# A decoder layer in one pass over 16 batches: where the choice of tokens and the turning of the context stand in a batch

## The chip, the cores and the metric

One Trainium2 chip, one core of it. The metric is the device time of the whole kernel in microseconds. The kernel before was timed in three runs. Engines are named as in the profile: PE is the matmul engine, DVE the vector engine, ACT the scalar engine, POOL the GpSimd engine, SP the engine that here issues only DMAs.

## The reference

The input x has 16 batches of 256 tokens of 128 numbers; the context has 16 batches of 1601 keys of 96 numbers. Three blocks follow each other, each on a layernorm of x and added to x:

```python
x = x + attention(layernorm(x))                     # one head of 128, 256 tokens
x = x + cross_attention(layernorm(x), ctx_768)      # 16 heads of 64, 1601 keys
x = x + ffn(layernorm(x))                           # a block on chosen tokens only
```

The third block weighs each token by `weights = x @ router_w + router_b`, takes the top 32 of 256 (`topv, topi = top_k(weights, 32)`), and processes the best 31 of them (sorted by place) with a small attention of 16 heads of 8, rotary angles and an MLP of 512. The processed tokens, times their weight, are written back to their places. The other tokens pass through: `out + x * (1 - sel_mask)`.

Nearly all of the work is the cross attention: per batch and pair of heads, scores of 2 x 256 queries against 1601 keys, an exponential, and the weighted sum of the context.

## The kernel before

**Tiles.** A batch has 104 tiles: 8 pairs of heads times 13 tiles of 128 keys. A tile (step `st`) is a pair of matmuls on PE (L593, L594) that make 128 keys x 512 queries of scores, split in a high and a low fp16 part, and an exponential on ACT (L910) into `PF`. Two tiles together are then rounded to the high part `EH` (step `round`; three of four on DVE, L1100, the fourth on ACT, L917), and POOL takes the rest, `EL = PF - EH` (step `lo`, L1599). Eight tiles after the scores, step `av` multiplies both parts with the context, `Ch` and `Cl` (L610, L612), into one PSUM bank. After 13 tiles step `norm` on DVE divides by the sum (L1142, L1146) into `Un`. `PF` holds 10 tiles, `EH` and `EL` 12.

**Around the tiles.** The work of the other blocks and of the next batch is laid between the tiles:

- For the next batch the context is scaled (`ctx_max` L1198, `sigma` L1204 to L1215, `ctx_scale` L962), split in `Ch` (ACT, L970) and `Cl` (DVE, L1225), and both are turned by a DMA of SP into `ChT` and `ClT` (step `turn_c`, L1716). Step `keys` (DVE, L1119) takes differences between the turned keys into `KD`.
- For each half head of queries a bound of the scores is found in advance: `diff` and `base` on PE (L634), a relu on ACT (L923), `fold` on DVE (L1126). One stands every three tiles. `base` and `fold` share two PSUM banks, so the next `base` waits for the `fold` before. `placemax` (PE L673, ACT L957, a DMA of SP, L1709) puts the bounds into a row of `AH`.
- `q` (PE L644, ACT L944, DVE L1135) makes the queries of a pair of heads 38 tiles ahead.
- The self attention of the next batch stands at tiles 5 to 56.
- The normalised sums are split, copied, turned by DMA (`u_split` L930, `u_copy` L1695, `u_low` L1605 on POOL's own DMA queue, `turn_u` L1700) and projected (`proj`, PE L655, DVE L1186).
- **Choice of tokens of the batch before**: `ln_stats2` and `sel_w` (DVE, tiles 26 to 31) make the layernorm and the weights. `sel_row` (PE, L776) turns the weights into a row in PSUM. Two `sel_count` steps on DVE (one for each half of the tokens: L1391 twice, L1393 once) count how many weights are larger. `sel_rank` (DVE, L1401, L1403, L1410, L1414) makes the ranks, the choosing matrix `GT` and adds the layernormed token to `X` where it is not chosen.
- The block on the chosen tokens runs once for four batches, in 22 steps at the tiles `CHOSEN_PLACES` of the four batches that follow; its first, `c_gather`, stands at tile 82 of the first and needs `GT` of all four.

**What sets the order.** There is no scheduler at run time. `plan` gives each step a tile, `whole_order` makes the list of each engine by sorting by tile, and `LATER` shifts a kind of step on one engine. Each engine works through its list in order and waits on semaphores where a step needs another engine. SP's list is its DMA queue: it too works in order. Small results on PE share one PSUM bank, number 7: each such step waits until the one before it has been read (`bank_free`, `freed`); `sel_row` holds it until both counts are done, `proj` until L1186.

Of the kernel before, what the change touches and what calls it, by code (L numbers as in the profile page):

```python
# [72 lines left out]
def self_attention(b):  # L73
    return [(k, b) for k in ("ln_stats0", "ln0", "sa_t", "sa_qk", "sa_v", "sa_s", "sa_turn", "sa_o",
                             "ln_stats1", "sa_n2", "sa_f")]
# [10 lines left out]


SA_PLACES = (5, 7, 10, 12, 30, 32, 56)
SEL_PLACE = 35
KEYS_LATER = 16  # L90
SIGMA_PLACE = 72
M_PLACE = 34
SPLIT_LATER, COPY_LATER, LOW_LATER, TURN_LATER, PROJ_LATER = 1, 2, 5, 9, 18
# [47 lines left out]
def ahead(n):  # L141

    if n == 0:
        todo = [(max(KT * hp - Q_LEAD, 5 * hp - 5), ("q", n, hp)) for hp in range(2, HP)]
        groups = FIRST_HEADS
    else:
        todo = [(KT * hp - Q_LEAD, ("q", n, hp)) for hp in range(HP)]
        firsts = [(h, KT * h // 2) for h in range(0, H, EARLY)]
        groups = [(h, h + EARLY, k - MAX_LEAD, k - ROW_LEAD - 3, k - ROW_LEAD) for h, k in firsts]
    for h0, h1, start, end, row in groups:  # L150

        for k, ht in spread(range(T * h0, T * h1), start, end):
            todo += zip((k, k + 1, k + 1), maximum(n, ht))
        todo += [(row, ("placemax", n, h0, h1))]
    return todo


def plan(b, beside):

    n = b + 1  # L160
    todo = [(k, step) for k, step in ahead(b) if k >= 0]
    if b >= 1:
        after = AV_LAG + KT + 5
        todo += [(after, ("ln_stats2", b - 1)), (after + 2, ("sel_w", b - 1)), (SEL_PLACE, ("sel_row", b - 1)),
                 (SEL_PLACE - 1, ("sel_count", b - 1, 0)), (SEL_PLACE + 3, ("sel_count", b - 1, 1)),
                 (SEL_PLACE + 13, ("sel_rank", b - 1))]
    if b == 0:
        todo += [(M_PLACE, ("m_max",)), (M_PLACE + 2, ("mtop",)), (M_PLACE + 5, ("msplit",))]
        todo += [(9, ("ln_stats0", 1)), (12, ("ln0", 1))]
        todo += [(10 + 4 * x, ("load_x", x)) for x in range(2, B)] + [(72, ("load_rest",))]  # L170
        todo += [(10, ("ctx_max", 1)), (18, ("sigma", 1)), (22, ("ctx_scale", 1))]
    if b == 1:
        todo += [(90, ("gains",))]
    if b + 2 < B:
        todo += [(SIGMA_PLACE - 14, ("ctx_max", b + 2)), (SIGMA_PLACE, ("sigma", b + 2)),
                 (SIGMA_PLACE + 1, ("ctx_scale", b + 2))]
        todo += [(97, ("ln_stats0", b + 2)), (101, ("ln0", b + 2))]
    if n < B:
        todo += [(TILES + k, step) for k, step in ahead(n) if k < 0]
        split = AV_LAG + 17 * (b == 0)  # L180
        todo += [(split - 3, ("ctx_hi", n, 0)), (split + 1, ("ctx_hi", n, 1))]
        todo += [(split + 1, ("ctx_lo", n, 0)), (split + 4, ("ctx_lo", n, 1))]
        todo += [(split + 8, ("turn_c", n, 0)), (split + 10, ("turn_c", n, 1)), (split + KEYS_LATER, ("keys", n))]
        q = [k + 9 * (b == 0) for k in SA_PLACES]
        todo += list(zip((*q[:6], q[5] + 4, q[5] + 9, q[6]), self_attention(n)[2:]))
        todo += [(q[6] + 2, ("bias", n))]
    return sorted(todo + beside.get(b, []), key=lambda x: x[0])
# [26 lines left out]
def whole_order(engine):  # L214
# [9 lines left out]
    for n in range(TOTAL + AV_LAG):  # L224
        b, k = n // TILES, n % TILES
        if k == 0 and b < B:
            todo = plan(b, groups)
        if k == AV_LAG + (29 if b == 0 else 12) and b + 2 < B:
            put(n, "load_ctx", b + 2)
        if n < TOTAL:  # L230
            put(n, "st", n)
        late = n - AV_LAG
        if late >= 2 and late % KT == 2:
            put(n, "av", late - 2)
            put(n, "av", late - 1)
        if late >= 0 and late % KT >= 2:
            put(n, "av", late)
        if late >= 0 and late % KT == KT - 1 and late // KT < B * HP - 1:
            put(n, "norm", late // KT)
        if n % 2 and ROUND_LAG <= n < TOTAL + ROUND_LAG:  # L240
            put(n, "round", n // 2 - ROUND_LAG // 2)
        if n % 2 and LO_LAG <= n < TOTAL + LO_LAG:
            put(n, "lo", n // 2 - LO_LAG // 2)
        while todo and todo[0][0] <= k and b < B:
            put(n, *todo.pop(0)[1])
        done = n - AV_LAG - (KT - 1)
        if done >= 0 and done % KT == SPLIT_LATER:
            put(n, "u_split", done // KT)
        for later, kind in ((COPY_LATER, "u_copy"), (LOW_LATER, "u_low"), (TURN_LATER, "turn_u"), (PROJ_LATER, "proj")):
            since = done - KT - later  # L250
            if since >= 0 and since % (2 * KT) == 0:
                quad = since // (2 * KT)
                put(n, kind, quad // QD, quad % QD)
# [1509 lines left out]
```

## Time and profile before

| | us |
|---|---|
| three runs | 2188.89, 2190.83, 2190.88 (median 2190.83) |
| profiled execution, own time | 2186.77 |
| its span | 2185.5 |
| PE busy | 2026.2 |
| POOL busy | 1881.3 |
| DVE busy | 1795.1 |
| ACT busy | 1754.8 |

The span is the time from the first to the last instruction in the profile. The busy time of PE is an upper figure, since matmuls overlap and their ends are modelled. The granted clock of PE is 0.992 of full speed over the span. Times given with an instruction are counted from the start of the span. A number in square brackets in a row of the timeline is the time that the engine was idle just before it, with what ended the idle time.

### The profile page before, as it was taken

Reading aid. Unit: us, or ns where it says so; the run is one execution under the profiler, and the core shown is the slowest. Engines: PE = TensorE matmul, PEld = TensorE weight load, DVE = VectorE, ACT = ScalarE, POOL = GpSimd, SP = SyncE. Lnnn points to the kernel's source line nnn. Section 1 sums busy time; section 2 is a strip of 40 time slices with the busy share of each in tenths; the row PEclk is TensorE's granted clock in tenths of the full one; section 3 lists DMA queues with packets and bytes.
Section 4 is the critical chain, followed back from the end, with each engine's and each line's share of the span. In section 5 each row is a group of like instructions: output and inputs, shape, how many; then the busy total and the mean of one; then the engine's idle time right before and its main releaser. Section 6 shows DMA issues by size and latency. Waiting matters only on the chain.

```text
span 2185.5 us, 56667 instructions
## 1 busy us (share of the span) xinstructions
PE 2026.2 (93%) x21333; PEld 1325.7 (61%) x21333; DVE 1795.1 (82%) x4371; ACT 1754.8 (80%) x2940; POOL 1881.3 (86%) x1066
## 2 busy tenths in 40 slices
PE   8899999999999999999999999999999999999997
PEld 4566566666666556666566666666665665666653
DVE  7788889798887888888797898988879788897864
ACT  6888888888887788888788788888878778888871
POOL 4798998989898888989888888898988889889990
PEclk9999999999999999999999999999999999999999
DMA  3222121121211112121131210312121121211111
GB/s 74 64 67 51 30 45 32 27 58 30 47 27 35 40 31 50 25 56 30 26 58 23 51 31 20 55 31 47 27 48 39 27 47 27 46 23 24 30 40 25
DMA packets 189262, 85.44 MB, mean 39 GB/s; under 512 B 161344, under 2 KB 186816, under 8 KB 188992
## 3 DMA queue, kind: packets, MB, share of 16 engines
q1 hardware_dynamic: 178672, 69.04, 14.9%
q0 software_dynamic: 9216, 12.59, 4.9%
q8 instruction: 171, 2.80, 0.5%
q14 instruction: 99, 0.81, 0.1%
q10 hardware_dynamic: 1104, 0.20, 0.1%
HBM read 16.46 MB, written 2.10 MB: 8 GB/s over the span
## 4 chain that ended last, share of the span: by engine, by line
PE 51%; DVE 21%; ACT 14%; issue 9%; POOL 4%; DMA 0%; DVEq 0%; ACTq 0%; POOLq 0%
PE PS L593 10%; PE PS L634 9%; PE PS L610 9%; PE PS L594 8%; PE PS L612 8%; DVE EH L1100 8%; ACT PF L910 6%; DVE over L1126 5%; POOL EL L1599 4%; ACT over L923 3%; ACT EH L917 2%; PE PS L644 2%; PE PS L655 1%; DVE KD L1119 1%; ACT ex L986 1%
## 5 line engine op out<-in xcount | busy, mean ns | idle before, releaser
L1599 POOL TENSOR_TENSOR EL<-PF,EH 128x1024 f16<-128x1024 f32 x828 | 1767.8, 2209 | 225.8 <-DVE EH L1100 93.8
L910 ACT ACTIVATE PF<-PS 128x512 f32<-128x512 f32 x1664 | 975.3, 600 | 239.1 <-PE PS L594 226.5
L610 PE MATMUL PS<-Ch,EH 128*128 128x97 f16 (+1 forms) x6656 | 751.8, 207 | 30.2 <-POOL EL L1599 27.8
L610 PEld LDWEIGHTS PS<-Ch,EH 128*128 128x128 f16 (+1 forms) x6656 | 605.3, 98 | 251.5 <-issue 95.5
L1100 DVE TENSOR_SCALAR_CACHE_REDUCE EH<-PF 128x1024 f16<-128x1024 f32 x621 | 748.7, 1210 | 8.5 <-ACT PF L910 8.5
L612 PE MATMUL PS<-Cl,EL 128*128 128x97 f16 (+1 forms) x6656 | 748.6, 207 | 0.0
L612 PEld LDWEIGHTS PS<-Cl,EL 128*128 128x128 f16 (+1 forms) x6656 | 596.3, 98 | 150.2 <-issue 3.2
L1126 DVE CUSTOM_DVE_ANT_1 over<-over,PS 128x802 f32<-128x802 f32 x512 | 505.5, 987 | 210.1 <-PE PS L634 124.4
L593 PE MATMUL PS<-AH,ChT 98*128 98x512 f16 x1664 | 637.6, 383 | 37.1 <-ACT PF L910 36.4
L594 PE MATMUL PS<-AL,ClT 96*128 96x512 f16 x1664 | 634.7, 381 | 0.0
L923 ACT ACTIVATE over<-PS 128x802 f32<-128x802 f32 x512 | 431.3, 842 | 57.2 <-PE PS L634 34.7
L593 PEld LDWEIGHTS PS<-AH,ChT 98*128 98x128 f16 x1664 | 162.7, 98 | 190.8 <-ACT PF L910 118.6
L634 PE MATMUL PS<-ChT,AH 96*128 96x401 f16 x1024 | 261.6, 336 | 10.6 <-DVE pmax L1126 10.3
L634 PE MATMUL PS<-KD,AH 96*128 96x401 f16 x1024 | 260.6, 335 | 1.5 <-ACT over L923 1.2
L917 ACT ACTIVATE EH<-PF 128x1024 f16<-128x1024 f32 x211 | 222.8, 1056 | 0.0
L594 PEld LDWEIGHTS PS<-AL,ClT 96*128 96x128 f16 x1664 | 164.2, 99 | 67.3 <-issue 0.9
L1135 DVE SCALAR_TENSOR_TENSOR AL<-PS,qscale,AH 96x512 f16<-96x512 f32 x128 | 95.3, 744 | 43.5 <-ACT AH L944 43.5
L944 ACT ACTIVATE AH<-PS,qscale 96x512 f16<-96x512 f32 x128 | 88.1, 689 | 33.6 <-PE PS L644 32.8
L644 PE MATMUL PS<-X2T,G 128*96 128x256 f16 x512 | 80.2, 280 | 22.5 <-DVE X L1186 15.2
L634 PEld LDWEIGHTS PS<-ChT,AH 96*128 96x128 f16 x1024 | 79.4, 99 | 32.1 <-DVE pmax L1126 15.8
L634 PEld LDWEIGHTS PS<-KD,AH 96*128 96x128 f16 x1024 | 80.4, 99 | 21.8 <-ACT over L923 3.5
L930 ACT ACTIVATE UHL<-Un 128x384 f16<-128x384 f32 x128 | 67.6, 528 | 16.9 <-DVE Un L1146 16.8
(261 smaller groups left out, 1572.4 us busy)
## 6 DMA issues: line engine op xcount, KB each, us to landing
UHL<-UHL SPq DMA_DIRECT2D x64, 192.0 KB, 2.2
UHL<-Un POOLq DMA_DIRECT2D x64, 192.0 KB, 3.5
Cf<-in_ctx SPq DMA_DIRECT2D x16, 576.0 KB
X<-in_x SPq DMA_DIRECT2D x16, 128.0 KB, 2.3
out_x<-X SPq DMA_DIRECT2D x16, 128.0 KB, 1.8
UT<-UHL SPq DMA_TRANSPOSE x64, 3.7
msk<-in_attention_mask SPq DMA_DIRECT2D x4, 256.0 KB, 4.4
AH<-mh SPq DMA_DIRECT2D x63, 2.0 KB
```

Of the source, the lines that this page charges most:

```text
L593: pe.matmul(o, ChT[j][0:DC + 2, t, :], AH[:, cs], start=True, stop=False)
L594: pe.matmul(o, ClT[j][0:DC, t, :], AL[:, cs], start=False, stop=True).then_inc(sg("st"), 1)
L610: pe.matmul(PS[:, 6, u0:u0 + DC + 1], EH[0:kr, r, qs], Ch[j][0:kr, t, 0:DC + 1], start=(t == 0 and q == 0), stop=False, skip_group_check=True)
L612: m = pe.matmul(PS[:, 6, u0:u0 + DC + 1], EL[0:kr, r, qs], Cl[j][0:kr, t, 0:DC + 1], start=False, stop=(t == KT - 1), skip_group_check=True)
L634: m = pe.matmul(PS[:, bank + n, 0:NKEY], AH[0:DC, ht * P:(ht + 1) * P], src[:, n * NKEY:(n + 1) * NKEY], start=True, stop=True)
L644: m = pe.matmul(PS[0:DC, kb, j * S:(j + 1) * S], G[:, part, 2 * hp + j, :], X2T[:, part, b % 2, :], start=(part == 0), stop=(part == 1))
L910: act.activation(PF[:, n % PRING, :], PS[0:KP, 4 + n % 2, :], ACT.Exp).then_inc(sg("ex"), 1)
L917: act.activation(EH[:, r - 1:r + 1, :], PF[:, f - 1:f + 1, :], ACT.Copy, scale=KEEP).then_inc(sg("eh_act"), 1)
L923: act.activation(over[:, i % 2, :, :], PS[:, 2:4, 0:NKEY], ACT.Relu).then_inc(sg("relu"), 1)
L1100: dve.tensor_scalar(EH[:, r - 1:r + 1, :], PF[:, f - 1:f + 1, :], KEEP, None, ALU.mult, ALU.add, accum_out=esum[:, r // 2:r // 2 + 1]).the ...
L1126: dve.tensor_tensor_reduce(out=o, in0=o, in1=PS[:, 0:2, 0:NKEY], scale=1.0, scalar=LEAST, op0=ALU.add, op1=ALU.max, accum_out=pmax[:, b % ...
L1599: pool.tensor_tensor(EL[:, r - 1:r + 1, :], PF[:, f - 1:f + 1, :], EH[:, r - 1:r + 1, :], ALU.subtract).then_inc(sg("lo_pool"), 1)
```

## The change

Two constants and two offsets in `plan` are changed. `sel_row` goes from tile 35 to 60, the two counts from 34 and 38 to 59 and 63 (on DVE one later: 35 and 39 to 60 and 64), `sel_rank` from 48 to 73. `turn_c` goes from tiles 16 and 18 to 13 and 15, and `keys` from 24 to 21 (in batch 0, which has 17 more, from 33, 35 and 41 to 30, 32 and 38). No instruction is added or removed.

```diff
-SEL_PLACE = 35
-KEYS_LATER = 16
+SEL_PLACE = 60
+KEYS_LATER = 13
...
-        todo += [(split + 8, ("turn_c", n, 0)), (split + 10, ("turn_c", n, 1)), (split + KEYS_LATER, ("keys", n))]
+        todo += [(split + 5, ("turn_c", n, 0)), (split + 7, ("turn_c", n, 1)), (split + KEYS_LATER, ("keys", n))]
```

`SEL_PLACE` is read by four steps:

```python
todo += [(after, ("ln_stats2", b - 1)), (after + 2, ("sel_w", b - 1)), (SEL_PLACE, ("sel_row", b - 1)),
         (SEL_PLACE - 1, ("sel_count", b - 1, 0)), (SEL_PLACE + 3, ("sel_count", b - 1, 1)),
         (SEL_PLACE + 13, ("sel_rank", b - 1))]
```

## Rows read from the trace of the kernel before

**Rows 1.** The page, part 1: busy time, share of the span, instructions.
```profile
PE 2026.2 (93%) x21333; PEld 1325.7 (61%) x21333; DVE 1795.1 (82%) x4371; ACT 1754.8 (80%) x2940; POOL 1881.3 (86%) x1066
```

**Rows 2.** The page, part 4: the chain that ended last, by engine.
```profile
PE 51%; DVE 21%; ACT 14%; issue 9%; POOL 4%; DMA 0%; DVEq 0%; ACTq 0%; POOLq 0%
```

**Rows 3.** Stretches of batch 2: length, then PE, PEld, DVE, ACT, POOL busy (instructions).
```profile
331.20:337.50 6.30, 5.14 (x58) 3.63 (x57) 5.37 (x11) 4.72 (x8) 4.60 (x3) 1.00 0.00 1
...
349.10:363.10 14.00, 12.42 (x124) 7.40 (x122) 13.04 (x40) 11.00 (x21) 13.83 (x10) 1.00 0.28 43
...
378.00:390.80 12.80, 11.85 (x136) 7.67 (x135) 9.56 (x19) 11.12 (x21) 12.80 (x8) 1.00 0.34 62
```

**Rows 4.** Timeline of POOL in batch 2: start, us, instruction, times [idle before].
```profile
323.54 10.50 POOL L1599 TENSOR_TENSOR EL<-PF,EH 128x1024 f16<-128x1024 f32 x5 [0.87 <-DVE EH L1100]
335.75 2.13 POOL L1599 TENSOR_TENSOR EL<-PF,EH 128x1024 f16<-128x1024 f32 x1 [1.70 <-ACT PF L910]
...
359.92 6.53 POOL L1599 TENSOR_TENSOR EL<-PF,EH 128x1024 f16<-128x1024 f32 x3
368.16 8.42 POOL L1599 TENSOR_TENSOR EL<-PF,EH 128x1024 f16<-128x1024 f32 x4 [1.71 <-ACT EH L917]
...
394.99 4.23 POOL L1599 TENSOR_TENSOR EL<-PF,EH 128x1024 f16<-128x1024 f32 x2 [0.20 <-PE PS L612]
399.70 6.50 POOL L1599 TENSOR_TENSOR EL<-PF,EH 128x1024 f16<-128x1024 f32 x3 [0.48 <-DVE EH L1100]
```

**Rows 5.** Timeline of DVE around the keys, in batch 0 (first row) and 2.
```profile
100.83 0.56 DVE L1119 TENSOR_TENSOR KD<-ChT 96x802 f16<-96x802 f16 x1
...
329.10 1.21 DVE L1100 TENSOR_SCALAR_CACHE_REDUCE EH<-PF 128x1024 f16<-128x1024 f32 x1
...
331.68 0.99 DVE L1126 CUSTOM_DVE_ANT_1 over<-over,PS 128x802 f32<-128x802 f32 x1 [1.36 <-PE PS L634]
...
332.60 1.88 DVE L1119 TENSOR_TENSOR KD<-ChT 96x802 f16<-96x802 f16 x1
```

**Rows 6.** Timeline of DVE at the ranking of batch 2.
```profile
364.38 0.21 DVE L1401 TENSOR_SCALAR_CACHE_REDUCE rank<-cnt 128x1 f32<-128x1 f32 x1
...
365.18 1.43 DVE L1414 SCALAR_TENSOR_TENSOR X<-X,keep 128x128 f32<-128x128 f32 x1
...
366.54 0.34 DVE L1414 SCALAR_TENSOR_TENSOR X<-X,keep 128x128 f32<-128x128 f32 x1
...
366.81 1.21 DVE L1100 TENSOR_SCALAR_CACHE_REDUCE EH<-PF 128x1024 f16<-128x1024 f32 x1
```

**Rows 7.** Groups by line, over the span: busy us, mean ns | idle before.
```profile
L634 PE MATMUL PS<-ChT,AH 96*128 96x401 f16 x1024 | 261.6, 336 | 10.6 <-DVE pmax L1126 10.3
...
L1391 DVE TENSOR_SCALAR_CACHE_REDUCE junk<-PS,X 128x256 bf16<-128x256 f32 x64 | 27.9, 473 | 0.8 <-PE PS L776 0.8
```

**Rows 8.** Timelines of DVE, SP, PE at the turning in batch 2; UT to landing.
```profile
316.67 1.44 DVE L1225 SCALAR_TENSOR_TENSOR Cl<-Ch,Cf 128x576 f16<-128x576 f16 x1
...
316.45 1.48 SPq L1716 DMA_TRANSPOSE ChT<-Ch  x1
321.91 1.44 SPq L1700 DMA_TRANSPOSE UT<-UHL  x1
...
324.24 1.91 SPq L1716 DMA_TRANSPOSE ClT<-Cl  x1
...
332.16 0.22 PE L655 MATMUL PS<-MH,UT 128*128 128x128 f16 x1
...
UT<-UHL SPq DMA_TRANSPOSE x64, 3.7
```

**Rows 9.** Timeline of DVE at tiles 70 to 77 of batch 2.
```profile
389.68 0.99 DVE L1126 CUSTOM_DVE_ANT_1 over<-over,PS 128x802 f32<-128x802 f32 x1 [2.12 <-PE PS L634]
...
394.77 0.98 DVE L1126 CUSTOM_DVE_ANT_1 over<-over,PS 128x802 f32<-128x802 f32 x1
...
397.43 0.99 DVE L1126 CUSTOM_DVE_ANT_1 over<-over,PS 128x802 f32<-128x802 f32 x1 [1.66 <-ACT over L923]
```

## The prediction

> **What bounds the kernel now.** I read the busy shares first, then the chain of waits, then one batch cut into stretches, then single instructions there. PE is busy in 93% of the span, POOL 86%, DVE 82% [rows 1], and the chain has 51% on PE, 21% on DVE, 14% on ACT [rows 2]: no engine is the bound throughout, so a place must be read by itself. I use batch 2 (its tile 0 is at about 302 us); batches 1 to 14 repeat it, those with steps of the chosen tokens with some longer gaps. The reader is to see in [rows 3] that the limit changes inside a batch. At tiles 60 to 72 POOL is busy for all of 12.80 us and DVE for 9.56: the pass on POOL that makes the low parts (EL), 2.1 us for each pair of tiles, sets the pace, and DVE has 3.2 us to spare. At tiles 24 to 28 it is the other way: 6.30 us for 4 tiles, with POOL busy for 4.60. Every idle gap of POOL is time which its queue of passes cannot get back, so I price the change by POOL's gaps. Batch 2 has one of 1.70 us at tile 27 and one of 1.71 us at tile 52 [rows 4]. The first follows the key differences (KD), the second the ranking (sel_rank); both stand in DVE's queue ahead of the rounding (EH) that POOL's next pass reads. In batches 1 to 14 the first is 1.7 us, and 2.3 us in five of them (5, 7, 9, 11, 13); the second is 1.71 to 2.0 us in batches 1 to 15.
>
> **Keys three tiles sooner.** KD is issued at 332.60 and takes 1.88 us; alone, with POOL idle, it took 0.56 [rows 5]. It ended at 334.48, 0.44 us after POOL's pass of that moment (323.54 + 10.50 = 334.04 [rows 4]). So it waits for POOL's pass and then needs 0.44 us. At tile 21 KD stands ahead of the rounding that begins at 329.10. POOL's fourth pass of the row of five ends at about 331.9, its third at 329.9. I take it that KD gets in at 329.9 and ends at 330.3; that rounding ends at 331.5, and POOL's fifth pass is held from 331.9 to 332.4 and ends at 334.5. The fold at 331.68 waited 1.36 us for PE [rows 5], so DVE had that much room; the next rounding, no longer behind KD, ends at 333.8. POOL's next pass begins at 334.5, not 335.75: 1.25 us gained in each of 14 batches, 17.5 us, and 0.6 us more in the five with the longer gap, 3 us. Bounds for a batch: 1.70 if nothing new appears, 0 if KD has to let one more pass go first (then KD ends at 332.4 and the rounding it holds at 333.6).
> [...] The row shows 0.56 alone against 1.88 beside a pass. [...] No row shows DVE waiting while POOL has its next EL pass ready.
>
> **Context turned sooner.** SP doesn't go by tiles, it goes by its queue. ChT already follows the split at once (316.45), since nothing of its queue stands between it and the wait; moving it from 16 to 13 changes no order. ClT does change: it stood behind the turning of UT (321.91) and the row maxima, and left at 324.24, though the split ended at 316.67 + 1.44 = 318.1 [rows 8]. It will leave at about 318, and the context load behind it can only go sooner. UT, now behind it, waits for the accumulation on POOL's queue; were it late by a whole issue (1.9 us), or by all 6.1 us that ClT gains, it would still be ahead of its reader or just there: the projection reads UT at 332.16, issue to landing of UT is 3.7 us, 321.91 + 3.7 = 325.6, so 6.6 us are free [rows 8]. I take 0; bounds 0 and 6.1 - 6.6, also 0. KD needs ChT alone, which landed some 9 us before 329.10.
>
> **Ranking away from tile 48.** Its instructions begin at 364.38; the addition to X (L1414) takes 1.43 us and 0.34 us, and the rounding behind it begins at 366.81, so 2.43 us [rows 6]. Again the first addition ends (366.61) 0.16 us after POOL's pass (359.92 + 6.53 = 366.45 [rows 4]). With it gone the rounding runs 364.4 to 365.6, POOL goes on at 366.5 in place of 368.16: 1.71 us gained, in 15 batches 25.7 us. Bounds 1.71 and 0.9 (if PE, busy 93%, sets a pace of its own there); I take 1.71, the gap itself.
>
> **Counting away from tiles 35 to 39.** Four comparisons of 0.473 us [rows 7] and two instructions of the same width, which I put at the same, are 2.8 us, 1.4 for each half, and a little less as they follow each other closely: 1.3. In tiles 36 to 48 POOL is busy 13.83 of 14.00 us [rows 3], so DVE's relief there gives nothing by itself; bounds 0 and 0.2. At the new place (tiles 60 and 64) DVE has 3.2 us spare in 12.80. The first count holds one rounding by 1.3 us where POOL has about 1.0 us of work in hand: 0.3 us lost. The second is taken up by the idle 2.12 us ahead of 389.68 [rows 9]. The q matmuls of tile 66 share bank 7 and now wait for the second count; they read it some 0.6 us later, with q needed 38 tiles ahead. Bounds 0 and 2.6; I take 0.3.
>
> **Ranking at tile 73.** This is the dear one. It lands behind sigma, the normalisation and a rounding, ahead of the fold at 394.77 [rows 9]. Small parts 0.8 us, to 395.6; the first addition waits for the pass begun at 394.99, to 397.1, and ends at 397.3, the second at 397.6: 2.8 us. The fold then ends at 398.5, PE's next base matmuls (0.336 us each, two that overlap [rows 7]: about 0.4) wait for it, the next fold runs 398.9 to 399.9 where it was 397.43, and the rounding ends at 401.05 rather than 399.55. POOL's pass of 399.70 [rows 4] starts at 401.1: 1.4 us lost. DVE's idle 1.66 us ahead of 397.43 has paid for the rest. Bounds 0 (the idle time covers it all) and 3.5 (one pass more to wait for, 2.1 us). Batch 15 has no folds, so 14 batches: (1.4 + 0.3) x 14 = 23.8 us lost.
>
> **Sum.** -17.5 - 3.0 - 25.7 + 23.8 = -22.4 us. Against the profiled execution's own 2186.77 us (span 2185.5, the rest lies around it) that is 2164.4. The median of the three runs is 4.1 us higher, 2190.83; from there 2168.4, and I say 2169.
>
> **Rivals.**
> A. The ranking at 73 is hidden whole, as is the counting: -46.2 us, 2145. For it: DVE idles 2.12 and 1.66 us around it [rows 9]. Against: that idle time lies on both sides of the cluster and not in it.
> B. The gains don't add: PE, busy 5.14 of 6.30 us at tiles 24 to 28 but 11.85 of 12.80 at 60 to 72 [rows 3], fills up when POOL's gaps close, or KD gives nothing and the rest cancels: -22.4 + 20.5 = -2, 2189.
> C. [...] In the new places POOL's passes stand back to back (five in a row from 323.54 and two from 394.99 [rows 4]), while at both old places POOL ran dry behind the instruction. If DVE has to let the next pass go first, the ranking costs 2.13 us more in 14 batches (+30 us) and KD's gain goes (+20.5): +28, 2219. With it in the ranking alone +7.5, 2198. It decides as soon as one addition in the ranking takes over 2 us. Against: at both old places DVE got in 0.16 and 0.44 us after the pass.
>
> **Chances.** Forecast 0.55 (its own range 2158 to 2182), A 0.12, B 0.13, C 0.20. The range takes in most of A, B, and C in the ranking alone: 2148 to 2202. About 0.2% (4.4 us) is what a measurement of this kernel can tell from no change. Faster 0.68 (forecast, A and a little of B), same 0.12, slower 0.20.
>
> **What would show it.** Right: POOL's gap at tile 27 under 0.6 us and none at tile 52; the first addition of the ranking at 1.4 to 1.9 us; a new gap of POOL of 1.5 to 2 us at tile 78 to 80; tiles 24 to 56 shorter by about 3 us, tiles 60 to 80 longer by under 2. Wrong: KD over 2.5 us, or an addition over 2 us (C); the gaps gone and the batch as long as before (B); no new gap near 79 (A). The forecast falls if the cluster at 73 makes PE wait for bank 7, where the projection of tile 77 must be added before q at 79, beyond the 1.4 us counted.

## The result and the profile after

The changed kernel took 2255.52 us (median of 4 runs, 2253.59 to 2259.72), the kernel before 2190.85 in the same comparison: ratio 1.030, 95% interval 1.0282 to 1.0318. It is 65 us slower, where 22 us faster was forecast. The profiled execution is 2253.59 us with a span of 2252.3. One execution in all the runs below, of kernel 7, had a granted clock of 0.653 and took 2865.65 us; it is left out of that kernel's time.

First the page: busy time, and the chain by engine. They answer to [rows 1, 2].

```profile
PE 2055.9 (91%) x21333; PEld 1343.6 (60%) x21333; DVE 1822.1 (81%) x4371; ACT 1747.0 (78%) x2940; POOL 1887.9 (84%) x1066
...
PE 48%; DVE 23%; ACT 14%; issue 10%; POOL 4%; DMA 1%; SPq 0%; ACTq 0%; DVEq 0%; POOLq 0%
```

PE's mean granted clock is new: 0.975 of full speed, 0.992 before. The page can't say more. Batch 2 in stretches can (the columns are those of [rows 3], then the granted clock of PE); these are tiles 24 to 28, 48 to 52, 52 to 60, 60 to 64, 72 to 76 and 76 to 80.

```profile
336.70:342.40 5.70, 5.70 (x68) 4.03 (x65) 4.57 (x13) 4.50 (x8) 5.59 (x4) 1.00 0.02 4
...
367.20:372.00 4.80, 4.80 (x67) 3.60 (x66) 4.05 (x11) 3.86 (x7) 4.80 (x3) 1.00 0.02 3
372.00:381.60 9.60, 9.60 (x104) 6.58 (x102) 8.18 (x16) 8.76 (x15) 9.15 (x6) 1.00 0.01 2
381.60:385.50 3.90, 3.62 (x46) 2.34 (x45) 3.90 (x12) 3.40 (x7) 2.87 (x3) 1.00 0.15 53
...
394.80:401.30 6.50, 5.28 (x56) 3.00 (x55) 6.25 (x26) 6.06 (x9) 6.32 (x4) 1.00 0.01 3
401.30:411.10 9.80, 6.69 (x57) 4.74 (x58) 7.07 (x14) 3.74 (x7) 5.42 (x3) 0.83 0.01 2
```

Tiles 24 to 28 are 0.60 us shorter than in [rows 3], as wanted. Tiles 76 to 80 took 4.20 us before and take 9.80: the loss is in these four tiles, and it repeats: 9.8 to 12.6 us in batches 1 to 14, where they took 4.2 to 4.9 before. Summed over these batches they take 145.7 us for 59.7; the next largest loss is 4.3 us, at tiles 64 to 72. The same instructions on DVE (start, us):

```profile
334.72 1.19 DVE L1119 TENSOR_TENSOR KD<-ChT 96x802 f16<-96x802 f16 x1
...
398.82 0.21 DVE L1401 TENSOR_SCALAR_CACHE_REDUCE rank<-cnt 128x1 f32<-128x1 f32 x1
...
399.62 1.69 DVE L1414 SCALAR_TENSOR_TENSOR X<-X,keep 128x128 f32<-128x128 f32 x1
401.24 2.20 DVE L1414 SCALAR_TENSOR_TENSOR X<-X,keep 128x128 f32<-128x128 f32 x1
403.37 0.98 DVE L1126 CUSTOM_DVE_ANT_1 over<-over,PS 128x802 f32<-128x802 f32 x1
405.40 0.99 DVE L1126 CUSTOM_DVE_ANT_1 over<-over,PS 128x802 f32<-128x802 f32 x1 [1.05 <-PE PS L634]
406.32 1.21 DVE L1100 TENSOR_SCALAR_CACHE_REDUCE EH<-PF 128x1024 f16<-128x1024 f32 x1
```

KD takes 1.19 us, not 1.88 [rows 5]. The second addition to X takes 2.20 us, not 0.34 [rows 6]. The ranking is 4.55 us long (398.82 to 403.37); before it was 2.43. POOL, then PE at the end of its wait:

```profile
329.16 12.94 POOL L1599 TENSOR_TENSOR EL<-PF,EH 128x1024 f16<-128x1024 f32 x6 [0.95 <-DVE EH L1100]
...
357.86 19.06 POOL L1599 TENSOR_TENSOR EL<-PF,EH 128x1024 f16<-128x1024 f32 x9
...
385.40 2.14 POOL L1599 TENSOR_TENSOR EL<-PF,EH 128x1024 f16<-128x1024 f32 x1 [1.03 <-ACT PF L910]
...
399.03 4.26 POOL L1599 TENSOR_TENSOR EL<-PF,EH 128x1024 f16<-128x1024 f32 x2 [0.18 <-PE PS L612]
407.67 4.25 POOL L1599 TENSOR_TENSOR EL<-PF,EH 128x1024 f16<-128x1024 f32 x2 [4.38 <-DVE EH L1100]
```

```profile
404.41 0.85 PE L634 MATMUL PS<-ChT,AH 96*128 96x401 f16 x2 [4.12 <-DVE pmax L1126]
```

Both old gaps of POOL [rows 4] are gone: six passes and nine passes stand back to back. In their place is one gap of 4.38 us. Where two passes follow each other from 399.03, the first addition ends at 401.31, 0.15 us after a pass, and the second at 403.44, 0.15 us after the next. That next pass began at about 401.12, while the first addition was ending and 0.12 us before the second was issued (401.24); it is so in batches 1 to 13 alike. The fold is then read by PE at 404.41, after 4.12 us in which PE, whose queue has the base matmuls first, does nothing. In short stretches behind that wait the clock is:

```profile
402.50:404.00 1.50, 0.00 (x0) 0.00 (x0) 1.50 (x3) 0.00 (x0) 0.79 (x1) 1.00 0.00 0
404.00:406.00 2.00, 1.59 (x6) 0.68 (x7) 0.95 (x3) 0.00 (x0) 0.00 (x0) 0.60 0.00 0
406.00:408.00 2.00, 2.00 (x22) 1.94 (x21) 1.54 (x4) 0.60 (x1) 0.33 (x1) 0.54 0.00 0
408.00:410.00 2.00, 2.00 (x26) 1.43 (x24) 1.62 (x3) 1.43 (x3) 2.00 (x2) 1.00 0.03 8
```

PE stood still for 4.12 us and was then granted half: in stretches of 0.5 us the clock is 0.50 from 404.5 to 407.5, 0.68 in the next and 1.00 from 408.0 on. Over the span, PE's waits for the fold ahead of the base matmuls are 68.5 us in 29 waits; before they were 10.3 in 15.

The turning did what was said. ClT leaves ahead of UT, UT leaves 0.8 us later in its batch, and PE's waits for it are what they were: one, of 6.1 us. SP's queue (it answers to [rows 8]):

```profile
322.06 1.48 SPq L1716 DMA_TRANSPOSE ChT<-Ch  x1
323.75 3.13 SPq L1716 DMA_TRANSPOSE ClT<-Cl  x1
328.33 1.44 SPq L1700 DMA_TRANSPOSE UT<-UHL  x1
```

### The profile page after: what moved, and what is told of

Its sections match the earlier page's. It is cut to its first block, busy times and chain, and to the rows that moved or that the text cites. A ratio compares the mean times of both kernels' runs of the same rounds, so it can differ in the third digit from the quotient of the medians.

```text
span 2252.3 us, 56667 instructions
## 1 busy us (share of the span) xinstructions
PE 2055.9 (91%) x21333; PEld 1343.6 (60%) x21333; DVE 1822.1 (81%) x4371; ACT 1747.0 (78%) x2940; POOL 1887.9 (84%) x1066
## 3 DMA queue, kind: packets, MB, share of 16 engines
q1 hardware_dynamic: 178672, 69.04, 14.9%
## 4 chain that ended last, share of the span: by engine, by line
PE 48%; DVE 23%; ACT 14%; issue 10%; POOL 4%; DMA 1%; SPq 0%; ACTq 0%; DVEq 0%; POOLq 0%
PE PS L593 9%; PE PS L634 8%; PE PS L594 8%; PE PS L610 8%; PE PS L612 7%; DVE EH L1100 7%; ACT PF L910 5%; DVE over L1126 4%; POOL EL L1599 4%; ACT over L923 3%; DVE X L1414 3%; ACT EH L917 2%; PE PS L655 2%; PE PS L644 2%; DVE Un L1146 1%
## 5 line engine op out<-in xcount | busy, mean ns | idle before, releaser
L1599 POOL TENSOR_TENSOR EL<-PF,EH 128x1024 f16<-128x1024 f32 x828 | 1774.3, 2230 | 284.9 <-DVE EH L1100 149.4
L610 PE MATMUL PS<-Ch,EH 128*128 128x97 f16 (+1 forms) x6656 | 759.5, 208 | 34.4 <-POOL EL L1599 29.7
L612 PE MATMUL PS<-Cl,EL 128*128 128x97 f16 (+1 forms) x6656 | 756.3, 208 | 0.0
L612 PEld LDWEIGHTS PS<-Cl,EL 128*128 128x128 f16 (+1 forms) x6656 | 601.7, 99 | 153.6 <-issue 10.5
L593 PE MATMUL PS<-AH,ChT 98*128 98x512 f16 x1664 | 645.1, 388 | 34.4 <-ACT PF L910 33.2
L594 PE MATMUL PS<-AL,ClT 96*128 96x512 f16 x1664 | 641.7, 386 | 0.0
L634 PE MATMUL PS<-ChT,AH 96*128 96x401 f16 x1024 | 264.8, 340 | 68.8 <-DVE pmax L1126 68.5
L634 PE MATMUL PS<-KD,AH 96*128 96x401 f16 x1024 | 261.9, 337 | 1.5 <-ACT over L923 1.2
L634 PEld LDWEIGHTS PS<-ChT,AH 96*128 96x128 f16 x1024 | 79.1, 99 | 92.3 <-DVE pmax L1126 76.0
L634 PEld LDWEIGHTS PS<-KD,AH 96*128 96x128 f16 x1024 | 80.8, 99 | 21.7 <-ACT over L923 3.4
L644 PE MATMUL PS<-X2T,G 128*96 128x256 f16 x512 | 78.9, 277 | 11.7 <-DVE junk L1393 4.8
```

Source lines behind the costliest of these rows:

```text
L593: pe.matmul(o, ChT[j][0:DC + 2, t, :], AH[:, cs], start=True, stop=False)
L594: pe.matmul(o, ClT[j][0:DC, t, :], AL[:, cs], start=False, stop=True).then_inc(sg("st"), 1)
L610: pe.matmul(PS[:, 6, u0:u0 + DC + 1], EH[0:kr, r, qs], Ch[j][0:kr, t, 0:DC + 1], start=(t == 0 and q == 0), stop=False, skip_group_check=True)
L612: m = pe.matmul(PS[:, 6, u0:u0 + DC + 1], EL[0:kr, r, qs], Cl[j][0:kr, t, 0:DC + 1], start=False, stop=(t == KT - 1), skip_group_check=True)
L634: m = pe.matmul(PS[:, bank + n, 0:NKEY], AH[0:DC, ht * P:(ht + 1) * P], src[:, n * NKEY:(n + 1) * NKEY], start=True, stop=True)
L644: m = pe.matmul(PS[0:DC, kb, j * S:(j + 1) * S], G[:, part, 2 * hp + j, :], X2T[:, part, b % 2, :], start=(part == 0), stop=(part == 1))
```

## The experiments

Theory: because the two additions read two operands in SBUF, DVE waits for POOL's passes; at tile 75 these stand back to back and each addition waits for one (1.69 and 2.20 us); the fold behind them holds PE (4.12 us), which then also loses its clock (0.50 of full speed). Rivals: the cluster at tile 73 is too long whatever the additions do; the earlier DMA costs; the two parts collide. The texts on record call the theory, and that wait for POOL, "the port": that is a name and nothing more. The runs show which instructions were held beside POOL's passes and for how long, not what the two engines share.

The kernel before was timed again in each comparison, with medians from 2188.06 to 2190.85 us. Differences between kernels of different comparisons are therefore good to some 3 us; those against the kernel before are taken within one comparison.

**1. The keys and the turning alone.** From the changed kernel:

```diff
-SEL_PLACE = 60
+SEL_PLACE = 35
```

> The turning of the context at 13 and 15 and the keys at 21, the choice of tokens left at 35 to 48. After the change KD takes 1.19 us instead of 1.88 and the gap of POOL at tile 27 is nearly gone, so this part alone should be worth what was forecast: 1.25 us in 14 batches and 3 us more, 20 us, so 2170. The rival (the earlier DMA of ClT is what costs) has this kernel slower than before, up to 2255.

2166.62 us, ratio 0.990 (0.9886 to 0.9919): 21.4 us faster than before (2188.06 in this comparison). This part of the forecast holds, in size too.

**2. The choice of tokens alone.** From the kernel before: `SEL_PLACE = 60`.

> The choice of tokens at 60 to 73, the turning and the keys left where they were. If the two parts add up, 2255.5 + 20 = 2276. In the profile both additions to X of the ranking (L1414) should again take 1.7 and 2.2 us at tile 75 and PE should wait about 4 us for the fold behind them. If instead it is the two parts together that collide, it is near before, 2190 or less.

2274.78 us, ratio 1.040 (1.0383 to 1.0414), 86.7 us slower; the additions take 1.69 and 2.20 us. The parts add up: 2188.1 - 21.4 + 86.7 = 2253.4. The collision is out.

**3. The additions with one operand from SBUF.** From the changed kernel:

```diff
-m = dve.scalar_tensor_tensor(out=X[..t..], in0=X3[..t, 0:D], scalar=keep[..t..], in1=X[..t..],
-                             op0=ALU.mult, op1=ALU.add, accum_out=spill())
+m = dve.tensor_scalar(X[..t..], X3[..t, 0:D], keep[..t..], None, ALU.mult, ALU.add, accum_out=spill())
```

> The whole change, but the two additions to X of the ranking read one operand from SBUF instead of two (X is overwritten by X3 times keep, its old value is left out), same shape, same place. Theory of the port (DVE waits for POOL's passes because it reads two operands): both take 0.34 us, the ranking 1.6 us instead of 4.6, PE waits 3 us less for the fold, and the time falls below before: 2150 to 2165. Rival (the cluster of sigma, normalisation, ranking and fold at tile 73 is too long by itself, or bank 7 holds PE): the additions are short but the time stays above 2225.

2172.03 us, ratio 0.993 (0.9912 to 0.9941). DVE, then POOL:

```profile
395.23 0.34 DVE L1414 TENSOR_SCALAR_CACHE_REDUCE X<-X,keep 128x128 f32<-128x128 f32 x1
...
395.50 0.34 DVE L1414 TENSOR_SCALAR_CACHE_REDUCE X<-X,keep 128x128 f32<-128x128 f32 x1
```

```profile
399.74 4.22 POOL L1598 TENSOR_TENSOR EL<-PF,EH 128x1024 f16<-128x1024 f32 x2 [0.88 <-DVE EH L1100]
```

Beside the same passes both take 0.34 us, and 83.5 us are gone. The gap of 4.38 us is 0.88 (L1598 here is L1599 elsewhere). The edit changes the instruction too, and not only what it reads. The changed kernel's own trace has the first instruction with one operand from PSUM in place of SBUF (its durations are the least, the median and the most, in ns):

```profile
L1186 DVE SCALAR_TENSOR_TENSOR X<-PS,pback,X x64: 475/482/485, 115.7 to 2212.9; 128x256 f32<-128x256 f32 x64
```

57 of these 64 were issued while a pass of POOL ran, and none took over 485 ns. With the 0.34 us above this points to the second operand in SBUF: the instructions with one were not held, the additions with two were. The cluster without its waits is no disaster; but the time is 7 us over the end of what was expected, so the move costs something beside these waits.

**4. PE kept busy while it waits.** From the changed kernel:

```diff
+STREAM_BUSY |= {("base", n, 2): 17 for n in range(2, B)}
```

> The whole change, with 17 idle matmuls of 512 columns (0.22 us each, 3.7 us) on PE ahead of the base matmuls that wait for the fold at tile 76, in batches 1 to 14, so that PE is busy while it waits. After the change the granted clock falls to one half for 3.4 or 6.8 us behind that wait in nearly every batch. If that fall is part of the price, the clock stays at 1.00 and 1.7 to 3.4 us of each batch come back: 2255 - 30 = 2225. If the fall costs nothing, since others are waited for then, the time stays at 2255 or a little over.

2225.76 us, ratio 1.017 (1.0156 to 1.0186). The stretch of about tiles 75 to 80 of batch 2, then PE at its wait (lines of this kernel are one higher: L635 is L634):

```profile
397.20:407.00 9.80, 9.34 (x84) 5.62 (x83) 8.60 (x14) 5.29 (x9) 5.74 (x4) 1.00 0.01 2
```

```profile
397.59 3.83 PE L565 MATMUL PS<-identb 128*128 128x512 f16 x17
401.88 0.52 PE L635 MATMUL PS<-ChT,AH 96*128 96x401 f16 x2 [0.46 <-DVE pmax L1127]
```

The additions take 1.69 and 2.20 us as before, the clock stays at 1.00, and 29.8 of the 83.5 us come back. So some 30 us of the loss are the clock, not the wait. The fillers themselves end 0.46 us before the base matmuls begin, so they cost little.

**5. The ranking one tile later.** `("sel_rank", b - 1)` at `SEL_PLACE + 14`.

> The whole change, but the ranking one tile later, at 74: DVE takes the fold of tile 73 ahead of it. Theory (the ranking of 4.6 us holds the fold, the fold holds the base matmuls of tile 76, and PE stands in its queue for 4 us and loses its clock): the base of tile 76 is no longer held, the additions still take 1.7 and 2.2 us or more, and only the next fold and POOL's pass behind the ranking are late: 2190 to 2220. Rival (what counts is that POOL runs dry behind a ranking of 4.6 us, whatever the fold does): near 2255.

2208.52 us, ratio 1.008 (1.0049 to 1.0113). DVE, then POOL:

```profile
393.81 0.98 DVE L1126 CUSTOM_DVE_ANT_1 over<-over,PS 128x802 f32<-128x802 f32 x1
...
395.51 0.79 DVE L1414 SCALAR_TENSOR_TENSOR X<-X,keep 128x128 f32<-128x128 f32 x1
...
396.24 2.21 DVE L1414 SCALAR_TENSOR_TENSOR X<-X,keep 128x128 f32<-128x128 f32 x1
```

```profile
400.64 4.21 POOL L1599 TENSOR_TENSOR EL<-PF,EH 128x1024 f16<-128x1024 f32 x2 [2.34 <-DVE EH L1100]
```

The fold now goes first, the second addition waits as long as ever, and 47 us are back. PE's waits for the fold are 10.5 us in 15 waits, as in the kernel before (the profiled execution is the fastest of the four, 2197.42 us). So what made a wait of 2 us so dear was that it stood ahead of the fold that PE needed. The edit changes one thing more: the first addition waits 0.90 us less, so the 47 us are not the place of the fold alone.

**6. The turning alone.** From the kernel before: `turn_c` at `split + 5` and `split + 7`.

> The kernel before with the turning of the context alone at 13 and 15. ClT leaves ahead of UT. As forecast it changes nothing: 2188, within 4 us. Rival: it is part of what the keys gained (ClT and the context load sooner), then 2180 or less, or it costs a little that the keys paid, then over 2195.

2188.72 us, ratio 0.9996 (0.9987 to 1.0005). It changes nothing, in either direction.

**7. The wait at the old place.** Kernel 1 with the edit of kernel 3.

> The turning and the keys three tiles sooner, the choice at 35 to 48, and the two additions to X of the ranking with one operand from SBUF (the old X is left out). It measures what the port costs at the old place: the first addition takes 0.34 us, not 1.43, so 1.1 us less in 15 batches if POOL's gap at tile 52 shrinks by as much: 2166 - 16 = 2150. If that gap is set by something else, 2166.

2151.16 us, ratio 0.982 (0.9798 to 0.9835): 15.5 us less than kernel 1, as 1.1 us in 15 batches. Against kernel 3, the same work without any of these waits, the new places cost 20.9 us. The two profiled executions (2174.58 and 2149.10 us) say where. Over batches 1 to 14, tiles 64 to 72, where the counts now stand, take 129.1 us in kernel 3 and 118.9 here. Tiles 76 to 80, behind the ranking, take 70.8 and 59.7. All other stretches together differ by some 4 us, and the counts' old place (tiles 36 to 48) by 0.1. At the new one PE waits for the second count, 4.8 us in 12 waits, since the matmuls of the queries (L644) need bank 7; here and in the kernel before they have no such wait. Behind the ranking it waits 0.91 us for the fold in each of batches 1 to 13.

**8. One addition only.** The changed kernel with `for t in range(1)` for the additions of batches 0 to 14; the second half of the tokens is left out.

> The whole change, with only the first of the two additions to X of the ranking (the second half of the tokens isn't added, in batches 0 to 14). The forecast priced the ranking at tile 73 with one wait for the port; the second addition was put at 0.34 us and took 2.2. If the second wait is the step that failed, the time falls by far more than 2.2 us a batch, since PE waits less and keeps its clock: 2172 (both additions without a wait) plus 1.35 us in 14 batches is 2191; 2215 if the clock still falls. If the first wait does the harm, it stays above 2225.

2206.51 us, ratio 1.008 (1.0046 to 1.0103); the addition takes 1.69 us, POOL's gap is:

```profile
401.55 4.24 POOL L1599 TENSOR_TENSOR EL<-PF,EH 128x1024 f16<-128x1024 f32 x2 [1.92 <-DVE EH L1100]
```

The second addition alone is worth 49.0 us. The time lies between the two that were expected, and the clock still falls (mean 0.983): PE waits 2.0 us for the fold in batches 1 to 13.

**9. The additions where POOL has run dry.** Kernel 1 with all of its work; the two additions become a step of their own (`add_kept`), on DVE behind `sel_w` of the next batch; batches 14 and 15 keep them in the ranking.

```diff
+if b >= 2: todo += [(AV_LAG + KT + 7, ("sel_add", b - 2))]     # "dve": {"sel_add": 3}
...
-for t in range(T): m = dve.scalar_tensor_tensor(...)
+if b >= B - 2: add_kept(b)
```

> All of the work, as in the kernel with the turning and the keys alone sooner (choice at 35 to 48), but the two additions to X of the ranking stand behind the weights of the next batch, at tile 31 of DVE, where POOL has run dry in every profile so far (1.98 us idle at tile 34). Theory of the port: both additions take 0.34 us there, POOL's gap at tile 52 (1.71 us) goes, the one at 34 grows by 0.6 to 0.7 us: about 1.0 us less in 14 batches, 2166.6 - 14 = 2152. Rival (an instruction on DVE costs what it takes wherever DVE is late): no gain, 2166.

2157.01 us, ratio 0.986 (0.9845 to 0.9875). POOL in this kernel (L1607 is L1599 elsewhere):

```profile
342.12 2.13 POOL L1607 TENSOR_TENSOR EL<-PF,EH 128x1024 f16<-128x1024 f32 x1 [2.52 <-DVE EH L1109]
...
350.61 19.21 POOL L1607 TENSOR_TENSOR EL<-PF,EH 128x1024 f16<-128x1024 f32 x9
```

Both additions take 0.35 us. POOL's gap at tile 34 is 2.52 us where it was 1.98, and the one at 52 is gone. Net 9.6 us less than kernel 1 (14 were expected), 31 us less than before with nothing left out: the fastest full kernel here.

**10. The same in the changed kernel.**

> The whole change with all of the work, its two additions to X likewise behind the weights of the next batch at tile 31. If the additions at tile 73 to 75 are the whole cause, the time is that of the kernel in which they had one operand from SBUF (2172), less 0.68 us of ranking at 73 that is gone, plus 0.68 us at tile 31: 2165 to 2178. If something else of the move costs too, over 2190.

2178.87 us, ratio 0.996 (0.9944 to 0.9969). Moving two instructions turns the change from 65 us slower to 9 us faster than before (2188.12). The time is 0.9 us over the end of what was expected. Against kernel 9 it is 21.9 us slower, near the 20.9 of 3 against 7. This one isn't free of the wait: the ranking in batch 15 keeps its additions, and the first takes 5.17 us, for 1.42 us in kernel 9.

## Why the prediction was wrong

- **Keys sooner, -20.5 us**: right. Measured -21.4 for keys and turning together; KD 1.19 us, where 1.2 was worked out (329.1 to 330.3), by the wait for one pass. That KD would get in behind the running pass, ahead of the next, was my estimate; no row showed it. In the changed kernel it was issued at 334.72, 0.72 us before the next pass began, and waited for the running pass alone; it is so in batches 1 to 14.
- **Turning, 0**: right (kernel 6).
- **Ranking away from tile 48, -25.7 us**: the mechanism half right, the size wrong. POOL's gap of 1.71 us did close. But PE is busy for all 9.60 us of tiles 52 to 60, and tiles 48 to 60 take 14.4 us for 14.9 before: 0.5 us, not 1.7. POOL, ahead of PE, waits for ACT's exponentials at 385.40 instead (1.03 us). Experiment 7, in which only the wait at the old place is gone, gained 1.0 us a batch. That is near my lower bound (0.9, PE's own pace), and I took the gap itself; rival B named this for the whole change, and it held for this step.
- **Counting, +0.3 us a batch**: too small. Kernel 3 against kernel 7 has 0.7 us a batch at tiles 64 to 72. I let the queries of tile 66 wait for the second count at no cost, because their result is needed 38 tiles later. But PE works in order: it stood in its queue, 0.4 us each time. In the change itself this is half hidden: against the kernel before, tiles 64 to 68 are some 0.6 us longer and 68 to 72 some 0.3 shorter.
- **Ranking at tile 73, +1.4 us a batch**: the step that failed. I let the first addition wait for the pass and put the second at the 0.34 us of [rows 6]. There POOL had run dry behind the first; here its next pass was ready and began 0.12 us before the second addition was issued, which then waited for all of it: 2.20 us. Experiments 3 and 8 show it: without the waits -83.5 us, without the second alone -49.0. The signs that I had named say the same: the first addition took 1.69 us, within the 1.4 to 1.9 of a right forecast; the second was over 2 us, the sign of rival C; and the new gap of POOL was 4.38 us, not 1.5 to 2.
- **What a wait there costs.** Rival C had the mechanism (a further pass, 2.13 us) at 30 us for the ranking. The wait did decide, as C said, when an addition took over 2 us; its price was mis-sized. PE stood in its queue for the fold (4.12 us), and then ran at the lower clock, worth 29.8 us by experiment 4. The sum followed DVE and POOL and had no term for either. C also took the gain of the keys away, which did not happen. It had 0.20, and for the ranking alone 2198; the range ended at 2202.
- **Batch 15, 0**: put at nothing because it has no folds. From its tile 0 to the end the span is 6.8 us longer (182.2 for 175.4), behind an addition of 5.17 us and with 17 us at the lower clock (3.4 before). Kernel 2 has the same addition there, none of that lower clock, and no loss. So the clock is the likelier cause; no run tests it.
- The sum in its own terms, in medians: keys -21.4; new places without the wait for POOL +20.9; the remainder, that wait at the new place less the one at the old, is 86.7 - 21 = 66 us (experiments 3 and 7 give 83.5 - 15.5 = 68). The forecast had -2 for both together.

What stays open: no run moved counting by itself, so its share of the 21 us of the new places (10 us at tiles 64 to 72, 11 us at 76 to 80) is read from two traces and not tested. It also stays open why the first addition got in right behind the running pass in batches 1 to 13 and not in 14 and 15 (see the last section).

## What to carry to other kernels

The additions of the ranking, on DVE with two operands in SBUF, took 0.34 to 0.37 us where no pass of POOL ran, and 1.69 and 2.20 us where its passes stood back to back. The second looked cheap in the kernel before (0.34 us behind a pass, [rows 6]) because POOL had nothing queued there. So price a moved instruction of this kind by what POOL has ready at the new place, where the additions here waited for the rest of a running pass, for a pass of 2.17 us that began 0.12 us before one was issued, or for more (the last section), and put it where POOL runs dry for another reason, as in experiment 9 (0.35 us each). Then look at what stands behind it in DVE's queue: here PE's next matmuls waited for that, which cost PE 4.12 us a batch and, behind it, its clock (29.8 us in all, by experiment 4).

## What the runs showed of the hardware

The wait for POOL was longer than one pass in two rankings of the changed kernel. The first addition of the one that stands in batch 14 took 4.76 us (DVE, then POOL):

```profile
2027.04 4.76 DVE L1414 SCALAR_TENSOR_TENSOR X<-X,keep 128x128 f32<-128x128 f32 x1
...
2031.73 0.34 DVE L1414 SCALAR_TENSOR_TENSOR X<-X,keep 128x128 f32<-128x128 f32 x1
```

```profile
2020.91 10.73 POOL L1599 TENSOR_TENSOR EL<-PF,EH 128x1024 f16<-128x1024 f32 x5
```

It was issued in the third of five passes and ended at 2031.80, 0.16 us after the fifth (2020.91 + 10.73 = 2031.64). Two passes that began after it was issued went ahead of it. The ranking in batch 15 shows 5.17 us. This repeats: the ranking in batch 15 takes 5.16 to 5.18 us in kernels 2, 4, 5, 8 and 10, all with the ranking at its new place.

Elsewhere in the changed kernel the order of issue fits who was held. In batches 1 to 13 KD was issued 0.72 us before the next pass began and got in before it (1.19 us), and so did the first addition, issued 1.50 us before (1.69 us); the second was issued 0.12 us after that pass had begun and waited for it (2.20 us). The two long ones do not fit. One thing differs in the trace: where a pass went ahead of a waiting addition, it began some 0.3 us before the running pass ended (0.04 in batches 1 to 13). Whether that is a cause isn't shown.

In the changed kernel PE's wait for the fold, of 4.1 to 4.5 us, was followed by 3.4 or 6.8 us at a granted clock of 0.50 in each of batches 1 to 14. With 17 idle matmuls in that wait (kernel 4) the clock behind it stayed at 1.00 in all 14, and 30 us of 2255 came back.
